# Eight expert groups' rows merged per group and added into a DRAM table by accumulating scatters, with the second attention's projection alone in the last matmuls

## What is computed

```python
xn = _layernorm(x)
x = x + _L1_attn_ref(xn, ...) + _L1_ffn_ref(xn, ...)

# _L1_attn_ref: attention of 16 small heads, attn (1024 x 256), then
out = attn @ weight_proj.T

# _L1_ffn_ref
probs = softmax(x @ Wr);  topw, topi = top_k(probs, 4)          # 32 experts, 4 per token
topw = topw / sum(topw)
shared = (silu(x @ Wsg) * (x @ Wsu) @ Wsd) * sigmoid(x @ Wse)
sel, w, tok = topi.reshape(-1), topw.reshape(-1), repeat(arange(T), 4)
pos, valid = place in its expert's list, pos < 32               # 32 slots per expert
xe = zeros((32, 32, 256)).at[sel, posc].add(x[tok] * valid)
ye = (silu(xe @ Wg) * (xe @ Wu)) @ Wd
out = shared.at[tok].add(ye[sel, posc] * (w * valid))
```

## Time and profile before

| | us |
|---|---|
| median of 3 runs | 428.70 |
| lowest and highest | 428.68, 429.19 |
| the profiled execution | 429.21 |
| its span, first to last instruction | 426.8 |
| PE busy | 419.8 (98%) |
| DVE busy | 310.9 (73%) |
| ACT busy | 247.5 (58%) |
| POOL busy | 168.6 (40%) |

### The profile page before, as it was taken

The page is one execution under the profiler, slowest core; times in us unless marked ns, Lnnn a source line. Parts: engine busy times, 40 slices in busy tenths (PEclk is TensorE's granted clock), DMA queues, the critical chain, the costliest instruction groups (busy, mean ns, idle before and its releaser), DMA issues.

```text
span 426.8 us, 8853 instructions
## 1 busy us (share of the span) xinstructions
PE 419.8 (98%) x3070; PEld 377.2 (88%) x3070; DVE 310.9 (73%) x910; ACT 247.5 (58%) x671; POOL 168.6 (40%) x293
## 2 busy tenths in 40 slices
PE   8999999999999999999999999999999999999997
PEld 8788879999999999999999999999997777567797
DVE  5967575787787888787877767657689994688442
ACT  4666741887868788777867786434314622563120
POOL 3520002645554554554554530102077007699200
DMA  7800020501010101010000000000099942899002
GB/s 214 303 2 1 2 76 25 198 1 51 2 51 0 51 2 51 2 52 1 2 0 3 2 2 0 27 14 12 26 321 300 307 115 88 236 305 279 9 14 86
DMA packets 37754, 34.45 MB, mean 81 GB/s; under 512 B 2448, under 2 KB 35920, under 8 KB 37712
## 3 DMA queue, kind: packets, MB, share of 16 engines
q1 hardware_dynamic: 37328, 32.85, 26.2%
q0 software_dynamic: 384, 1.05, 0.8%
HBM read 31.80 MB, written 2.10 MB: 79 GB/s over the span
## 4 chain that ended last, share of the span: by engine, by line
PE 92%; DVE 5%; ACT 2%; issue 1%; POOL 0%; POOLq 0%; DVEq 0%
PE bank L945 21%; PE bank L947 21%; PE bank L946 21%; PE bank L1116 5%; PE bank L1128 3%; PE bank L1107 3%; PE bank L1350 2%; PE bank L1317 2%; PE bank L1361 2%; PE bank L1362 2%; PE bank L1158 2%; PE bank L1337 2%; DVE OS L1859 1%; PE bank L1022 1%; PE bank L1266 1%; DVE arena L1499 1%
## 5 line engine op out<-in xcount | busy, mean ns | idle before, releaser
L587 POOL TENSOR_TENSOR arena<-arena,rinv 128x384 f32<-128x384 f32 x64 | 52.9, 828 | 81.0 <-DVE rinv L1629 81.0
L945 PE MATMUL bank<-XTl,WA 128*128 128x512 f32 (+1 forms) x126 | 52.0, 412 | 0.9 <-DVE arena L1499 0.8
L947 PE MATMUL bank<-XTh,WA 128*128 128x512 f32 (+1 forms) x126 | 49.1, 390 | 0.0
L946 PE MATMUL bank<-XTh,WA 128*128 128x512 f32 (+1 forms) x126 | 49.1, 389 | 0.0
L771 ACT ACTIVATE PT<-bank 128x256 fp32r<-128x256 f32 x64 | 24.5, 383 | 34.0 <-PE bank L1116 34.0
L1633 DVE TENSOR_TENSOR PT<-bank,PT 128x256 fp32r<-128x256 f32 x64 | 27.2, 425 | 18.8 <-ACT arena L772 18.8
L945 PE MATMUL bank<-WA,XTh 128*128 128x256 f32 x128 | 38.3, 299 | 0.0
L578 POOL CAST Q<-arena 128x128 fp32r<-128x128 f32 x64 | 18.7, 292 | 47.0 <-PE bank L947 47.0
L946 PE MATMUL bank<-WA,XTl 128*128 128x256 f32 x128 | 35.7, 279 | 0.0
L947 PE MATMUL bank<-WA,XTh 128*128 128x256 f32 x128 | 35.7, 279 | 0.0
L1621 DVE CUSTOM_DVE_ANT_0 arena<-bank,posm 128x128 f32<-128x128 f32 x64 | 18.1, 283 | 20.8 <-PE bank L947 20.8
(11 more groups left out here) (329 smaller groups left out, 1455.5 us busy)
## 6 DMA issues: line engine op xcount, KB each, us to landing
arena<-in_L_ffn_Wg SPq DMA_DIRECT2D x6, 704.0 KB, 7.8
arena<-in_L_ffn_Wu SPq DMA_DIRECT2D x6, 704.0 KB, 10.3
arena<-in_L_ffn_Wd SPq DMA_DIRECT2D x6, 512.0 KB, 7.2
arena<-in_L_attn_Wk SPq DMA_DIRECT2D x8, 256.0 KB, 2.6
arena<-in_L_attn_Wv SPq DMA_DIRECT2D x8, 256.0 KB, 3.2
arena<-in_L_attn_Wo SPq DMA_DIRECT2D x1, 2048.0 KB, 8.4
arena<-in_L_ffn_Wd SPq DMA_DIRECT2D x6, 192.0 KB, 7.6
arena<-in_L_attn_Wq SPq DMA_DIRECT2D x4, 256.0 KB, 4.7
```

What stands on the lines that cost most here:

```text
L587: pool.tensor_tensor(pr, pr, r[:, :, None].to_broadcast([P, 3, P]), ALU.mult).then_inc(s_p, 1)
L945: pe.matmul(dst, wh, xl, start=start, stop=False)
L946: pe.matmul(dst, wl, xh, start=False, stop=False)
L947: return pe.matmul(dst, wh, xh, start=False, stop=stop)
```

## The change

**Where rows meet.** There are no masks over all tokens, no `YE`, `YH`, `YL` and no `mix` steps. A DRAM table `expert_rows` of 1024 + 128 rows is set to zero by one store early in the kernel (from `ZR`, filled by POOL). For each group, ACT weights the output out of the bank (`YW`), PE multiplies it once by `SAME[g]` (128 x 128, 1 where two slots of the group hold the same token), so that each slot holds its token's sum over the group, ACT copies the result (`YZ`), and POOL scatters its 128 rows into the table with an accumulating indirect transfer. Only the first slot of each token in the group goes to the token's row; the others go to the 128 spare rows. `row_places` on DVE works out the row (`rank`), from `BEFORE` (`SAME` below the diagonal, by POOL).

**Order.** Scatter g waits until scatter g - 1 has landed (its semaphore is the gather's, counted on to 32). ACT's copy of group g waits for scatter g - 2, whose buffer it takes. Once the last one has landed, SP loads the table in four transfers, and DVE adds it to `X` (`add_rows`), tile by tile.

**The list.** The groups' steps come first, "sd" 5 to 7 last. The turning of `AO` is split in two halves ("ao" 0 and 1) and stands in the list, before down(7) and behind it. After the list PE has only the 48 matmuls of the projection, each token tile in a bank of its own. DVE does the value products of the last tile (`last_values`), POOL those of tiles 0 to 6. The shared down product has two banks in place of three, since bank 3 takes the merges. Two matmuls with a row of ones spread the slots' token numbers over all partitions.

The core of the diff:

```diff
@@ EXPERT_STEPS
-                 ("high", 0), ("up", 6), ("slots", 7), ("high", 3), ("low", 0), ("sd", 6), ("turn", 6), ("low", 3),
-                 ("sd", 7), ("add", 7), ("down", 6), ("mix", 0), ("mix", 1), ("up", 7), ("mix", 2), ("turn", 7),
-                 ("mix", 3), ("down", 7)]
...
+                 ("split", 6), ("up", 5), ("slots", 6), ("down", 4), ("sd", 4), ("merge", 4), ("turn", 5), ("up", 6), ("slots", 7),
+                 ("down", 5), ("values", 0), ("turn", 6), ("merge", 5), ("up", 7), ("down", 6), ("values", 1), ("turn", 7), ("merge", 6),
+                 ("ao", 0), ("down", 7), ("ao", 1), ("merge", 7), ("sd", 5), ("sd", 6), ("sd", 7), ("add", 7)]
...
+PV_STEPS = [("values", 0, 0, 1), ("values", 1, 0, 1), ("values", 2, 0, 2), ("scatter", 0), ("values", 3, 0, 2), ("scatter", 1),
+            ("values", 4, 0, 3), ("scatter", 2), ("values", 5, 0, 3), ("scatter", 3), ("values", 6, 0, 2), ("scatter", 4),
+            ("values", 6, 2, 4), ("scatter", 5), ("scatter", 6), ("scatter", 7)]
@@ SyncE
             load_kv(0)
+            sp.dma_start(expert_rows.rearrange("(g p) d -> p g d", p=P), ZR[:, None, :].to_broadcast([P, GR + 1, D])).then_inc(s_xs, 16)
...
+            sp.wait_ge(s_xg[GR - 1], 32)
+            for k in range(B):
+                sp.dma_start(YS[:, 2 * k:2 * k + 2], expert_rows[2 * P * k:2 * P * k + 2 * P].rearrange("(g p) d -> p g d", p=P)).then_inc(s_x[k], 16)
@@ GpSimd
-            pool.iota(IT, [[1, N]], base=0, channel_multiplier=0, allow_small_or_imprecise_dtypes=True).then_inc(s_it, 1)
+            pool.wait_ge(s_gt, 2)
+            pool.affine_select(out=BEFORE, in_=SAME, compare_op=ALU.is_gt, fill=0.0, base=0,
+                               pattern=[[0, GR], [-1, P]], channel_multiplier=1).then_inc(s_it, 1)
...
+            def scatter(g):
+                if g == 0:
+                    pool.wait_ge(s_rk, 1)
+                else:
+                    pool.wait_ge(s_xg[g - 1], 32)
+                pool.wait_ge(s_yr, g + 1)
+                pool.indirect_dma_start(expert_rows, bass.IndirectOffsetOnAxis(ap=rank[:, g:g + 1], axis=0), YZ[:, g % 2], None,
+                                        compute_op=ALU.add).then_inc(s_xg[g], 16)
@@ ScalarE
-            def y_high(n):
-                act.wait_ge(s_ye, n + 1)
-                nc.scalar.activation(YH[:, n], YE[:, n], ACT.Copy, scale=slot_w[:, n:n + 1]).then_inc(s_yr, 1)
+            def y_weighted(g):
+                act.wait_ge(s_dn, g + 1)
+                act.wait_ge(s_sw1, 1)
+                if g >= 2:
+                    act.wait_ge(s_mg, g - 1)
+                nc.scalar.activation(YW[:, g % 2], pb[7][:, 0:D], ACT.Copy, scale=slot_w[:, g:g + 1]).then_inc(s_ye, 1)
+
+            def y_merged(g):
+                act.wait_ge(s_mg, g + 1)
+                if g >= 2:
+                    act.wait_ge(s_xg[g - 2], 32)
+                nc.scalar.activation(YZ[:, g % 2], pb[3][:, 0:D], ACT.Copy).then_inc(s_yr, 1)
@@ TensorE
+                for half in range(2):
+                    ins = pe.matmul(pb[4 + half][:], onesr[0:1, :], TKr[0:1, 512 * half:512 * half + 512], start=True, stop=True)
+                    ins.then_inc(s_tt, 1)
...
+            def expert_merge(g):
+                pe.wait_ge(s_ye, g + 1)
+                if g >= 1:
+                    pe.wait_ge(s_yr, g)
+                pe.matmul(pb[3][:, 0:D], SAME[:, g], YW[:, g % 2], start=True, stop=True).then_inc(s_mg, 1)
...
-            def mix_groups(j, groups, start, stop):
-                dst, ts = mix_tile(j)
-                for g in groups:
-                    pe.matmul(dst, GT[g][:, ts], YH[:, g], start=start and g == groups[0], stop=False)
-                    ins = pe.matmul(dst, GT[g][:, ts], YL[:, g], start=False, stop=stop and g == groups[-1])
-                return ins
...
+            def final_tile(j):
+                dst, ts = pb[FINAL_BANK[j]][:, 0:D], slice(P * j, P * j + P)
                 for c in range(C):
-                    ins = mm3(dst, AOTh[:, c, ts], AOTl[:, c, ts], PJh[:, c], PJl[:, c], False, c == C - 1)
+                    ins = mm3(dst, AOTh[:, c, ts], AOTl[:, c, ts], PJh[:, c], PJl[:, c], c == 0, c == C - 1)
                 ins.then_inc(s_fo, 1)
@@ VectorE
-            def slot_mask(g):
-                nc.vector.tensor_scalar(GT[g][:], IT, slot_t[:, g:g + 1], None, ALU.is_equal).then_inc(s_gt, 1)
...
+            def same_token(half):
+                n = GR // 2
+                dve.wait_ge(s_tt, 2 + half)
+                nc.vector.scalar_tensor_tensor(out=SAME[:, 4 * half:4 * half + n], in0=pb[4 + half][:, 0:P * n].rearrange("p (g n) -> p g n", g=n),
+                                               scalar=1.0, in1=slot_t[:, 4 * half:4 * half + n, None].to_broadcast([P, n, P]),
+                                               op0=ALU.max, op1=ALU.is_equal).then_inc(s_gt, 1)
...
+            def add_rows(j):
+                dve.wait_ge(s_x[j // 2], 32)
+                ins = nc.vector.tensor_tensor(X[:, j], YS[:, j], X[:, j], ALU.add)
```

More of the change, by code:

```diff
@@ L925, in _ @@
                     nc.scalar.activation(ACTh[:, n - 1], ACTT[n - 1][:, N // 2:N], ACT.Copy).then_inc(s_adh, 1)
-                if what == "high":
-                    if n == 0:
-                        act.wait_ge(s_dn, 6)
-                        act.wait_ge(s_sw1, 1)
-                    for i in range(n, n + 3):
-                        y_high(i)
-                if what == "down" and n == 6:
-                    y_high(6)
-            y_high(7)
-            nc.scalar.activation(PJh[:], projT[:], ACT.Copy).then_inc(s_pjh, 1)
-            for f in range(4):
-                act.wait_ge(s_at, f + 1)
-                nc.scalar.activation(AOTh[:, f // 2, 512 * (f % 2):512 * (f % 2) + 512], pb[4 + f][:], ACT.Copy).then_inc(s_ac, 1)
+                if what == "down":
+                    y_weighted(n)
+                if what == "merge":
+                    y_merged(n)
+                if what == "ao":
+                    if n == 0:
+                        nc.scalar.activation(PJh[:], projT[:], ACT.Copy).then_inc(s_pjh, 1)
+                    for c in range(C):
+                        act.wait_ge(s_at, 2 * n + c + 1)
+                        nc.scalar.activation(AOTh[:, c, 512 * n:512 * n + 512], pb[ao_bank(c, n)][:], ACT.Copy).then_inc(s_ac, 1)
         @block.tensor
@@ L1313, in expert_up @@
                     pe.wait_ge(s_eh, g - 1)
+                else:
+                    pe.wait_ge(s_gt, g + 1)
                 for c in range(C):
@@ new lines, in row_places @@
+            def row_places():
+                dve.wait_ge(s_it, 4)
+                nc.vector.tensor_reduce(earlier[:], BEFORE, AX, ALU.add)
+                step(nc.vector.tensor_scalar(slot_d[:], slot_t[:], spare[:, 0:1], None, ALU.subtract))
+                step(nc.vector.scalar_tensor_tensor(out=slot_d[:], in0=earlier[:], scalar=0.0, in1=slot_d[:], op0=ALU.is_gt, op1=ALU.mult))
+                nc.vector.scalar_tensor_tensor(out=rank[:], in0=slot_t[:], scalar=-1.0, in1=slot_d[:],
+                                               op0=ALU.add, op1=ALU.subtract).then_inc(s_rk, 1)
@@ new lines, in last_values @@
+            def last_values(part):
+                j = NT - 1
+                for k in (0, 1) if part == 0 else (2, 3):
+                    dst = AO[:, j] if k == 0 else pvt2
+                    p, v = value_operands(j, k)
+                    step(nc.vector.tensor_tensor(dst.rearrange("p (g r d) -> p g r d", g=G1, r=4), p, v, ALU.mult))
+                    if k:
+                        ins = nc.vector.tensor_tensor(AO[:, j], AO[:, j], pvt2, ALU.add)
+                        if k == 3:
+                            ins.then_inc(s_pd, 1)
+                        else:
+                            step(ins)
@@ L1862, in add_shared @@
+            def add_rows(j):
+                dve.wait_ge(s_x[j // 2], 32)
+                ins = nc.vector.tensor_tensor(X[:, j], YS[:, j], X[:, j], ALU.add)
+                if j < 4:
+                    ins.then_inc(s_pa, 1)
+                else:
+                    step(ins)
             def add_shared(j):
@@ L1869, in add_rest @@
                 dve.wait_ge(s_fo, j + 1)
-                nc.vector.tensor_tensor(X[:, j], pb[j][:, 0:D], X[:, j], ALU.add).then_inc(s_pa, 1)
+                ins = nc.vector.tensor_tensor(X[:, j], pb[FINAL_BANK[j]][:, 0:D], X[:, j], ALU.add)
+                if j < 4:
+                    step(ins)
+                else:
+                    ins.then_inc(s_pa, 1)
             for what, n in EXPERT_STEPS:
@@ L1874, in _ @@
                     shared_product(n[0])
+                if what == "shared" and n == (11, 1):
+                    same_token(0)
+                    same_token(1)
                 if what == "table":
@@ L1899, in _ @@
                     scores_weighed(1)
-                if what == "mask":
-                    for g in n:
-                        dve.wait_ge(s_it, 4)
-                        slot_mask(g)
```

(3 more changed lines are left out.)

199 lines of the change are left out of this document (109 added, 90 removed).

## The result

| kernel | median us | runs | ratio to before (95%) |
|---|---|---|---|
| before | 428.94 | 428.68 to 429.69, 4 | |
| changed | 434.81 | 433.46 to 435.35, 4 | 1.0126 (1.0101 to 1.0150) |

The changed kernel is slower by 5.9 us, where 421.4 us were forecast. The profiled execution took 435.35 us for a span of 433.2, 13.7 us more than the 419.5 of the sum.

A forecast was written before the change was run, and what follows sets the result against it. It took a queue of PE matmuls to bound the kernel's end. After the change the scatters end last: 409.5 landed + 5.3 reads + 2.55 adds + 2.1 = 419.5 span, + 2.4 - 0.5 = 421.4 us; range 417.4 to 428.

The forecast's parts named there:

- the sum: Path of eight scatters in a row, then table reads, DVE's adds and the end: 419.5 us of span.
- L: Time from a scatter's issue to its landing and the next issue: 4.0 us, bounds 2.8 to 5.6.
- Rival 2: Slower: from the fourth on scatters wait for landings, each us of L costs five; 430.4 us at L = 6.0; chance 0.13.
- Weights stall: PE before up(7), waiting for the last group's weights, delayed by broadcasts and scatters: 4.6 us, 1.7 to 5.5.
- PE without the stall: PE's end without a new stall: 424.2 - 15.4 - 0.4 + 0.5 + 2.4 = 411.3 us.
- A merge: PE's f32 product of 128x128 by 256 columns, per group: 0.3 us each, 2.4 for eight.
- The removal of 15.8 us: PE's path loses 128 mixing matmuls, 15.4 us, and the first one's 0.4 us wait for DVE.
- signs: A PE gap before a merge or down product, released by ACT, would mean that scatters hold the expert groups.
- rival 4: PE loses its clock in the weights stall, adding 2 us to PE's path: 422.3 us; chance 0.05.
- The reads of the table: After the last landing SyncE reads the table back, four times 256 KB: 5.3 us, 4.9 to 7.2.
- the tail: After the reads, two row adds and four last adds on DVE, 2.55 us, and 2.1 to the end.
- Rival 1: PE's path ends last, with L below 3.5: 420.3 us with full stall, 417.4 with the smallest; chance 0.27.

The follow-up runs named there:

- noload: Changed kernel without loading the weights of groups 4 to 7 (these use those of groups 0 to 3): 428.43 us, 1.0000 of the kernel before.
- values: Changed kernel with POOL's attention value products of tiles 4 to 6 left out: 431.78 us, 1.0078 of the kernel before.
- tables: Changed kernel with two tables, for even and odd groups, scatter g waiting for g-2, and a buffer per group's merged rows: 424.96 us, 0.9924 of before.
- buffers: Changed kernel with a separate buffer for each group's merged rows, so ACT never waits for a landing: 434.27 us, 1.0134 of the kernel before.
- quick: Changed kernel with scatters that write instead of adding and without loading the weights of groups 4 to 7: 421.14 us, 0.9834 of the kernel before.
- plain: Changed kernel with scatters that write instead of adding, same order and waits: 425.12 us, 0.9924 of the kernel before.

## Why the prediction was wrong

**The step that failed: L.** It was one number, 4.0 us, for eight scatters, and it was used only where the engines are empty; for the first three steps the sum took POOL's value products as the limit, which gave scatter 3 at 388.5. As a number for empty engines 4.0 was good: the last landing took 3.87, and the next issue follows 0.3 behind. Beside the weights it was 8.7, 7.6 and 9.0. By points of the chain, against the sum (the last column is what each point adds to the miss):

| point | sum | trace | miss, new |
|---|---|---|---|
| scatter 3 issued | 388.5 | 398.16 | +9.7 |
| scatter 7 issued | 405.5 | 417.93 | +2.8 |
| scatter 7 landed | 409.5 | 421.80 | -0.1 |
| last wait for the table ended | 414.8 | 427.36 | +0.3 |
| DVE's last add ended | 417.35 | 430.64 | +0.7 |
| span | 419.5 | 433.2 | +0.4 |

The 9.7 come from landings of 8.0 and 7.0 us, and a third of more than 8 by its step of 9.0, in place of 4 (noload gives the pair for the first: 3.8 without the stream, 8.0 with it). The prediction had the evidence: a DMA share of 1.16 up to 390 and weights that took 10.6 us to land. It used both for what the scatters do to the weights, and not for what the weights do to the scatters. The 2.8 are POOL: an issue is 1.6 us and not 1.25, two scatters come behind products that end later (values won 2.1 us), and scatter 5 took 5.0 us to land.

**Rival 2** named the mechanism and the place, and had 0.13. Its formula put the price on the last five scatters, where the stream is over; those averaged 4.7. By the formula the span of 433.2 would be reached at L = 6.95, which none of those five had. A scatter was priced from gathers that ran in a stretch of their own: a full-stream price would have needed the 10.6 of a weight load as the nearest row.

**Weights stall, 4.6 us: didn't come.** The transfer of 10.6 us took 10.7 in the changed kernel, issued at the same 383.88, and 11.1 in tables. So the scatters held it up by 0.1 to 0.5 us, and not by the 2.5 of the sum. In the changed kernel up(7) is at 402.03, late for other reasons. In tables, where PE isn't held, it starts at 394.80, with its weights there since 394.76. It was also due 1.9 us later than the sum had it (392.9).

**PE without the stall: 411.3; in tables 414.4.** A merge moves the next matmul by 0.44 to 0.63 us (381.81 to 382.25, 394.17 to 394.80), not 0.3, which is 1.6 of the 3.1 us; 0.77 is PE's wait for POOL's value products. The rest, 0.7 us, I can't place. The removal of 15.8 us fits this balance; no run takes the mixing out alone.

**What lay off the path.** ACT's wait for landings and the gap before the down product were foreseen as signs, and are there. So is the half clock of rival 4, but behind a gap that comes from the landings and not from the weights. Buffers shows that they cost nothing while the chain is last. The reads of the table (5.6 for 5.3) and the tail were right within 1.4 us together; four row adds come after DVE's last wait for a read, not two.

**Rival 1.** In the changed kernel no link was under 3.5 us. In quick the last ones were, and there PE's path does end last, at 421.1 us, a little above the rival's 417.4 to 420.3.

**L's page.** By the fit in "DMA: Bandwidth & Descriptors" of the Trainium skill, the section on the anatomy of a GpSimd DMA, such a transfer takes an estimated 2.3 us; the 3.2 of the prediction put POOL's issue on top. Unloaded, from the start of the issue, this case has 2.4 us without accumulation, near the fit alone, and 3.8 to 3.9 with it; the measurement decides. Beside a full stream it has 5.7 to 6.5 and 7.0 to 8.2.

**Slips in the sum.** 0.5 + 2.4 + 4.6 is 7.5 us, not 7.3. And the bounds that are given for the scatters' share of the engines make a stall of 3.8 to 5.5 us; nothing in them leads down to 1.7. Neither moved the forecast, and the second only widened the range downwards.

**Still open.** Why scatter 5 took 5.0 us to land in the changed kernel and in noload (both with DMA engines almost idle) and 3.8 in values and in tables. Why PE's clock fell where it did. The change of order alone, without scatters, wasn't tried.

## What to carry to other kernels

A chain of transfers that each wait for the landing of the one before must be priced at the landing time of the stretch where it runs: beside a stream that fills the DMA engines a small transfer took twice as long as alone, and it took that once per link. If the links are independent but for one destination, give them two destinations: here that won 8.7 us of a chain of eight, for 3.4 us of extra adds. And finish tiles in an order that spreads the stores, since a shorter tail that releases them all at once was no faster.

## What the runs showed of the hardware

- An accumulating scatter of 128 rows of 1 KB: POOL 1.57 to 1.64 us (changed kernel), landing mostly 3.8 to 3.9 us on idle engines, once 5.0; the same as a plain write: 1.0 and 2.4, with two issues of 1.35 and 1.49 and one landing of 4.2 in plain.
- Beside a weight stream (share 1.15, 302 GB/s in the changed kernel) the first landing was 8.0 us with accumulation and 6.5 without (plain). With two scatters in flight (tables) each took about as long: 8.2, 7.9 and 7.8.
- PE's clock went to 0.50 at the end of 1.07 us of matmuls that followed a gap of 2.92 us (changed kernel), and within a gap of 7.02 us (buffers); gaps of 1.04 and 1.24 us with the same product between them (plain) left it at 1.00.
- In tables scatter 1 kept POOL 2.80 us instead of 1.6, and in noload 2.34. In both DVE was in the middle of its 128x1536 operation (376.7 to 378.6 and 376.6 to 378.4 us) when the scatter was issued (377.21, 377.55); in quick, where that operation began at 377.80, just behind the issue at 377.70, the plain write took 1.02. No run separates the two, so the cause is not shown.
